# Where the two halves of P x V are joined and scaled: in the attention stage on VectorE and GpSimd, or in the output stage on GpSimd

## What is computed

```python
q = rmsnorm(x @ wq_a.T) @ wq_b.T              # 32 heads, 64 plain + 64 rotated
kv = rmsnorm(ckv) @ wkv_b.T                   # ckv has 64 columns
scores = einsum('bqhd,bkhd->bhqk', q_full, k_full) * softmax_scale
attn = softmax(where(causal, scores, min))
out = einsum('bhqk,bkhd->bqhd', attn, v)      # P x V
return out.reshape(B, S, H * VD) @ wo.T       # output product
```

## Time and profile before

| | before |
|---|---|
| median of three runs | 1893.46 us (1892.46 to 1895.08) |
| the profiled execution's own time | 1895.1 us (it is the longest of the three) |
| its span | 1895.1 us; nothing lies around it |
| TensorE busy (matmuls) | 1803.7 us, 95% |
| VectorE busy | 1231.4 us, 65% |
| ScalarE busy | 1000.5 us, 53% |
| GpSimd busy | 877.8 us, 46% |
| granted TensorE clock, mean | 0.985 |
| DMA | 182.74 MB, mean 96 GB/s |

### The profile page before, as it was taken

One profiled execution on the slowest core, in us unless ns is written; L12 is line 12 of the kernel. 1 busy time (PEld: TensorE's weight loads), 2 busy tenths in 40 slices (PEclk: granted clock), 3 DMA queues, 4 the chain that ended last, 5 costly groups with the idle time before them and its releaser, 6 DMA issues. The chain is left out here.

```text
span 1895.1 us, 44298 instructions
## 1 busy us (share of the span) xinstructions
PE 1803.7 (95%) x15472; PEld 1422.9 (75%) x15472; DVE 1231.4 (65%) x2654; ACT 1000.5 (53%) x2137; POOL 877.8 (46%) x641
## 2 busy tenths in 40 slices
PE   5999969899999999999999999998999999989999
PEld 4788869877777777777777777775788888877887
DVE  5655358688898888889888888989521111125453
ACT  2221047788887888888787888877310100112110
POOL 3232112377777878777787878775000000014321
PEclk9999979999999999999999999999999999989999
DMA  6542162311212112121222212123742233224321
GB/s 217 193 156 100 67 173 94 84 62 44 86 59 78 57 62 80 57 80 40 85 69 68 69 51 82 55 86 113 249 151 89 94 100 115 67 87 158 130 89 59
DMA packets 111969, 182.74 MB, mean 96 GB/s; under 512 B 27680, under 2 KB 64672, under 8 KB 109856
## 3 DMA queue, kind: packets, MB, share of 16 engines
q1 hardware_dynamic: 111904, 181.88, 29.8%
HBM read 122.33 MB, written 59.51 MB: 96 GB/s over the span
## 5 line engine op out<-in xcount | busy, mean ns | idle before, releaser
L1290 PE MATMUL psS<-keyT,q 128*128 128x512 f32 (+2 forms) x2304 | 473.2, 350 | 23.9 <-POOL q L648 14.5
L1290 PEld LDWEIGHTS psS<-keyT,q 128*128 128x128 f32 x2304 | 381.2, 189 | 118.2 <-DVE negmax L1408 41.7
L1357 ACT ACTIVATE prob<-prob,negmax 128x640 f32<-128x640 f32 (+7 forms) x512 | 392.0, 767 | 78.5 <-DVE negmax L1408 75.9
L1418 DVE STREAM_TRANSPOSE pT<-prob 128x640 f32<-128x640 f32 (+7 forms) x512 | 379.9, 762 | 66.4 <-PE psV L1307 61.6
L1408 DVE CUSTOM_DVE_ANT_0 prob<-psS,mask 128x640 f32<-128x640 f32 (+7 forms) x512 | 371.9, 742 | 20.9 <-PE psS L1290 7.4
L469 PE MATMUL f_psy<-f_weff,f_xT 128*128 128x512 f32 x1344 | 315.6, 393 | 0.0
L1101 PE MATMUL psS<-o_w,o_o 128*128 128x512 f32 x1344 | 304.8, 389 | 0.0
L469 PEld LDWEIGHTS f_psy<-f_weff,f_xT 128*128 128x128 f32 x1344 | 250.9, 188 | 55.8
L1101 PEld LDWEIGHTS psS<-o_w,o_o 128*128 128x128 f32 x1344 | 252.3, 188 | 52.4
L1307 PE MATMUL psV<-pT,val 32*64 32x512 f32 (+3 forms) x8192 | 264.8, 407 | 6.4 <-DVE pT L1418 6.2
L1307 PEld LDWEIGHTS psV<-pT,val 32*64 32x64 f32 x8192 | 168.8, 132 | 109.7 <-issue 66.2
(11 more groups left out here) (120 smaller groups left out, 1919.1 us busy)
## 6 DMA issues: line engine op xcount, KB each, us to landing
wo<-in_wo SPq DMA_DIRECT2D x16, 1024.0 KB, 6.0
pT<-row_scales SPq DMA_DIRECT2D x128, 128.0 KB, 2.9
oT<-pT SPq DMA_DIRECT2D x64, 256.0 KB, 2.5
o_in<-oT SPq DMA_DIRECT2D x32, 512.0 KB, 5.2
f_xt<-in_x SPq DMA_DIRECT2D x16, 512.0 KB, 4.4
f_w_in<-in_w SPq DMA_DIRECT2D x16, 512.0 KB, 6.7
w_sum<-f_w_in SPq DMA_DIRECT2D x16, 512.0 KB, 5.3
x<-f_xo SPq DMA_DIRECT2D x16, 512.0 KB, 3.0
```

The lines of the kernel that those rows point to most:

```text
L1290: ins = nc.tensor.matmul(psS[:, slot, start + x0:start + x1], q[:, e, a, t * P:(t + 1) * P], k.keyT[:, m, b * S + x0:b * S + x1], start=(i ...
L1357: nc.scalar.activation(row, row, ACT.Exp, bias=negmax[:, n % 8:n % 8 + 1], scale=-1.0, accum_out=rowsum[:, column(n, s):column(n, s) + 1]) ...
L1418: nc.vector.transpose(pT[:, n % 2, t, 0:width], prob[:, n % RING, 0:width]).then_inc(turned, 1)
```

## The change

P x V's banks are copied whole, all 128 partitions, by ScalarE into o_raw, now four quarters of pT's free part, and this signals `evicted`. The joins on VectorE, the scalings on GpSimd and the way of the scales back into o_scale go. SP stores both partial sums in parts_d, 4 x 256 KB a unit, and the scales in a table by token tile. In the output stage, SP loads for each half tile the lower partial sums into o_in, the upper ones and the scales (spread over 64 partitions) into the not yet used low and high part of the tile's o: 12 transfers of 256 KB a tile. GpSimd adds and multiplies (`join_outputs`), and signals ScalarE. A tile's loads wait for the tile before to be split and for the one before that to be multiplied. o_in moves to the place of cosT and sinT, x_in to that of wo. The output product goes through the pairs in order with both banks of a pair together; tiles 0 and 1 are no longer laced. ScalarE and VectorE split weights 0 to 4 ahead of tile 0's first half; SP loads tile 1's outputs behind weight 13. All other jobs of the attention stage keep their order.

```diff
@@ -897,9 +897,9 @@
 ACT_STEP = ("F0-1 F1-1 E8-1 Q0+0 E9-1 E10-1 Q1+0 E11-1 W0-1 H0+0 E12-1 E13-1 H1+0 E14-1 E15-1 Q2+0 Q3+0 E0+0 E1+0 E2+0 "
             "E3+0 E4+0 E5+0 E6+0 H2+0 E7+0 H3+0 O0-1 O1-1 O2-1 O3-1")
 DVE_STEP = ("M15-1 T12-1 T13-1 M0+0 T14-1 M1+0 M2+0 M3+0 T15-1 M4+0 M5+0 T0+0 R1-1 T1+0 T2+0 M6+0 T3+0 M7+0 T4+0 T5+0 "
-            "T6+0 R0+0 T7+0 O0-1 M8+0 O1-1 F0+0 M9+0 O2-1 T8+0 F1+0 M10+0 M11+0 T9+0 O3-1 M12+0 M13+0 T10+0 T11+0 "
+            "T6+0 R0+0 T7+0 M8+0 F0+0 M9+0 T8+0 F1+0 M10+0 M11+0 T9+0 M12+0 M13+0 T10+0 T11+0 "
             "M14+0")
-POOL_STEP = ("B2+0 B3+0 A0+1 A1+1 B0+1 B1+1 P0-1 P1-1 A2+1 A3+1")
+POOL_STEP = ("B2+0 B3+0 A0+1 A1+1 B0+1 B1+1 A2+1 A3+1")
...
-        self.o_in = at("o_in", "wo", 0, [P, PAIRS, P])
+        self.o_in = at("o_in", "cosT", 0, [P, PAIRS, P])
         self.o = [at("o_o0", "qnT", row * SLOTS, [P, 2, PAIRS, P], F32R), at("o_o1", "val", 0, [P, 2, PAIRS, P], F32R)]
-        self.x_in = [at("o_x_in0", "cosT", 0, [P, D]), at("o_x_in1", "sinT", 0, [P, D])]
+        self.x_in = [at("o_x_in0", "wo", 0, [P, D]), at("o_x_in1", "wo", row, [P, D])]
...
-    def load_outputs(self, sp, n):
+    def raw(self, j, part, h):
+
+        return self.o[j][:, part, self.half_of(h), :].bitcast(F32).rearrange("p a n -> p (a n)")
+
+    def load_outputs(self, sp, n, j, h):
+        x = slice(h * PAIRS * P // 2, (h + 1) * PAIRS * P // 2)
+        parts = self.parts_d.rearrange("(n e h v) m -> e h v n m", n=NT, e=2, h=2)[:, :, :, bass.ds(n, 1), x]
+        for e in range(2):
+            rows = slice(KVR * e, KVR * e + KVR)
+            even, odd = (parts[e, i].rearrange("v a m -> v (a m)") for i in range(2))
+            scale = self.scales_v[e, bass.ds(n, 1), x].to_broadcast([KVR, PAIRS * P // 2])
+            sp.dma_start(self.o_in[rows, self.half_of(h), :].rearrange("p a n -> p (a n)"), even).then_inc(self.o_loaded[h], 16)
+            sp.dma_start(self.raw(j, LO, h)[rows, :], odd).then_inc(self.o_loaded[h], 16)
+            sp.dma_start(self.raw(j, HI, h)[rows, :], scale).then_inc(self.o_loaded[h], 16)
+
+    def join_outputs(self, nc, pool, n, j):
         for h in range(2):
-            sp.dma_start(self.o_in[:, self.half_of(h), :], self.oT_v[:, self.half_of(h), bass.ds(n * P, P)]).then_inc(self.o_loaded[h], 16)
+            both = self.o_in[:, self.half_of(h), :].rearrange("p a n -> p (a n)")
+            pool.wait_ge(self.o_loaded[h], n * 96 + 96)
+            nc.gpsimd.tensor_tensor(both, both, self.raw(j, LO, h), ALU.add).then_inc(self.o_joined, 1)
+            pool.wait_ge(self.o_joined, n * 2 + h + 1)
+            nc.gpsimd.tensor_tensor(both, both, self.raw(j, HI, h), ALU.mult).then_inc(self.o_scaled, 1)
+
+    def pool_steps(self, nc, pool):
+        for n in range(2):
+            self.join_outputs(nc, pool, n, n)
+
+        def step(n, j, has):
+            if has(1) and later(n, 1):
+                self.join_outputs(nc, pool, n + 1, (j + 1) % 2)
+        output_steps(pool, step)
...
                 sp.wait_ge(self.o_lo, n * 2 + 2)
-                self.load_outputs(sp, n + 1)
+                sp.wait_ge(self.product, n * 2)
+                for h in range(2):
+                    self.load_outputs(sp, n + 1, (j + 1) % 2, h)
...
-        act.wait_ge(self.o_loaded[h], n * 16 + 16)
+        act.wait_ge(self.o_scaled, n * 2 + h + 1)
...
-            if pair in (0, 1, 8, 9):
-                self.outputs_hi(nc, act, pair // 8, pair // 8, pair % 2)
+            if pair in (5, 7):
+                self.outputs_hi(nc, act, 0, 0, pair // 7)
...
-        behind = 8
-        for p in range(PAIRS + behind):
-            for tile, pair in ((0, p), (1, p - behind)):
-                if not 0 <= pair < PAIRS:
-                    continue
-                pe.wait_ge(self.o_lo, 2 * tile + 2 * pair // PAIRS + 1)
-                pe.wait_ge(self.w_lo, pair + 1)
-                for half in range(2):
-                    x = slice(half * BANK, (half + 1) * BANK)
-                    for i, (a, m) in enumerate(PASSES):
-                        ins = nc.tensor.matmul(self.ps[:, tile, x], self.o[tile][:, a, pair, :], self.w[pair][:, m, x],
-                                               start=(pair == 0 and i == 0), stop=(pair == PAIRS - 1 and i == 2))
-                    if pair == PAIRS - 1:
-                        ins.then_inc(self.product, 1)
+        def add_pair(j, pair, closing):
+            for half in range(2):
+                x = slice(half * BANK, (half + 1) * BANK)
+                for i, (a, m) in enumerate(PASSES):
+                    ins = nc.tensor.matmul(self.ps[:, j, x], self.o[j][:, a, pair, :], self.w[pair][:, m, x],
+                                           start=(pair == 0 and i == 0), stop=(pair == PAIRS - 1 and i == 2))
+                if closing:
+                    ins.then_inc(self.product, 1)
+
+        for pair in range(PAIRS):
+            pe.wait_ge(self.o_lo, 2 * pair // PAIRS + 1)
+            pe.wait_ge(self.w_lo, pair + 1)
+            add_pair(0, pair, pair == PAIRS - 1)
+        for pair in range(PAIRS):
+            pe.wait_ge(self.o_lo, 2 * pair // PAIRS + 3)
+            add_pair(1, pair, pair == PAIRS - 1)
...
+                for pair in range(PAIRS):
+                    if pair % (PAIRS // 2) == 0:
+                        pe.wait_ge(self.o_lo, n * 2 + 2 * pair // PAIRS + 1)
+                    add_pair(j, pair, pair == PAIRS - 1)
...
-            def turn_scales(it, ch, s):
+            def store_scales(it, ch, s):
 
                 step, x = it * 2 + s, 2 * QT * (s % 2) + QT * ch
-                rows = rinv_d[bass.ds(step, 1), ch * S:(ch + 1) * S].rearrange("a (c q) -> (a c) q", q=P)
                 sp.wait_ge(r_turned, step * 2 + ch + 1)
                 for g in range(BLOCKS):
-                    if g == BLOCKS - 1 and later(step, 1):
-                        sp.wait_ge(scaled, step * 2 + ch - 1)
-                    sp.dma_start(rows[:, 32 * g:32 * g + 32], rinvT[32 * g + x:32 * g + x + QT, x // QT, :]).then_inc(r_stored, 16)
-                sp.wait_ge(r_stored, step * 128 + ch * 64 + 64)
-                for e in range(2):
-                    x = ch * S + e * CHUNK
-                    sp.dma_start(o_scale[KVR * e:KVR * e + KVR, ch, :],
-                                 rinv_d[bass.ds(step, 1), x:x + CHUNK].to_broadcast([KVR, CHUNK])).then_inc(r_loaded[ch], 16)
-
-            def store_o(it, ch, s):
+                    sp.dma_start(rinv_d[x:x + QT, bass.ds((it + s // 2) * P + 32 * g, 32)],
+                                 rinvT[32 * g + x:32 * g + x + QT, x // QT, :]).then_inc(r_stored[x // QT], 16)
+
+            def store_o(it, e, s):
                 b, pair = s % 2, it + s // 2
-                sp.wait_ge(scaled, (it * 2 + s) * 2 + ch + 1)
-                sp.dma_start(oT_d[bass.ds(pair * P, P), b * S + ch * CHUNK:b * S + (ch + 1) * CHUNK], o_raw[:, ch, :]).then_inc(o_stored[ch], 16)
+                sp.wait_ge(evicted, (it * 2 + s) * 4 + 4)
+                parts = parts_d.rearrange("(n e p) m -> e p n m", n=NT, e=2)[e, :, :, bass.ds(pair * P, P)]
+                for a in range(2):
+                    n = b * QT + a * QT // 2
+                    sp.dma_start(parts[:, n:n + QT // 2, :],
+                                 o_raw[:, 2 * e + a, :].rearrange("p (t q) -> p t q", q=P)).then_inc(o_stored, 16)
...
-                        sp.wait_ge(w_done, units)
-                        sp.wait_ge(o_stored[0], 16 * (units - 1))
-                        output.load_outputs(sp, 0)
+                        sp.wait_ge(queries.roped, 4 * units)
+                        for ch in range(2):
+                            sp.wait_ge(r_stored[ch], 64 * PAIRS)
+                        sp.wait_ge(o_stored, 64 * (units - 1))
+                        for h in range(2):
+                            output.load_outputs(sp, 0, 0, h)
                     if r.last and s == 1 and job == "Z":
-                        sp.wait_ge(output.o_lo, 2)
-                        output.load_outputs(sp, 1)
-                        output.load_weights(sp, range(SLOTS, 3 * SLOTS))
+                        output.load_weights(sp, range(SLOTS, 2 * SLOTS))
                     if r.last and s == 1 and (job, n) == ("X", 1):
-                        output.load_weights(sp, range(3 * SLOTS, PAIRS))
+                        sp.wait_ge(w_stored, 16 * units)
+                        output.load_weights(sp, range(2 * SLOTS, 3 * SLOTS))
             rounds(sp, body)
-            sp.wait_ge(w_stored, 16 * units)
-            for ch in range(2):
-                sp.wait_ge(o_stored[ch], 16 * units)
+            output.load_weights(sp, range(3 * SLOTS, 14))
+            sp.wait_ge(output.o_lo, 2)
+            output.load_outputs(sp, 1, 1, 0)
+            output.load_weights(sp, range(14, PAIRS))
+            output.load_outputs(sp, 1, 1, 1)
+            for slot in range(4):
+                sp.wait_ge(r_stored[slot], 64 * PAIRS)
+            sp.wait_ge(o_stored, 64 * units)
...
```

(23 more changed lines are left out.)

72 lines of the change are left out of this document (28 added, 44 removed).

## The result

The changed kernel takes 1927.56 us (median of 4 runs, 1926.77 to 1929.93) against 1893.05 beside it: a ratio of 1.0181, 95% interval 1.0167 to 1.0196. It is slower by 34.5 us where 41 us of gain were forecast. Its profiled execution spans 1925.0 us, 29.9 more than that of before.

A forecast was written before the change was run, and what follows sets the result against it. TensorE was taken to bound the kernel, so time could be won only where it pauses or runs slowly. 36 + 3.3 + 2.3 - 0.7 = 40.9 us off 1893.5 gave 1852.5 us, range for 8 in 10 1838 to 1886.

The forecast's parts named there:

- The chain of the output stage: Output stage: a tile's load, join and split take 19.1 us, 21.0 at worst, under TensorE's 21.8, so cost nothing.
- third rival: Output stage: a tile's 4.2 MB at one low mean rate; at 242 GB/s 69 us lost, about 1921 us; chance 0.10.
- the ring: Output stage: load, join, split, then the next tile's loads, as o_in frees only after the split; put at 19.1 us.
- The attention stage's gain: Attention stage: 1.2 us a unit, 36 us over 30 intervals; low end 14 us, high end 48.
- (a): Attention stage: from P x V's end to the first query product 1.92 us instead of 2.71; about 0.8 with folds.
- (b): Attention stage: without scaling GpSimd's rotation starts 1.1 us earlier, just in time; up to 0.4 us wait every second unit.
- (c): Attention stage: VectorE, with 3.3 us less work, takes later maxima at once; 0.4 us a unit, ends 0 and 0.8.
- The wider evictions: Attention stage: ScalarE's whole-bank evictions stay at 0.59 us each; bounded at -0.1 and +0.2 us each.
- The last P x V: Change of stages: VectorE's joins leave the stretch before the last P x V; 3.3 us won (2 to 4).
- Tiles 0 and 1: Change of stages: waits and slow clock 5 us instead of 7.3; 2.3 us won (8 lost to 5 won).
- The last half result: End of the output stage: one half result falls behind the last matmul; 0.7 us lost (0 to 1.5).
- the prediction's second page: Skill page on DMA row pitch, 164 GB/s at 2 MiB: a unit's store about 6 us, tile 0 some 3 us later.

The follow-up runs named there:

- e1_wide: Changed kernel, output-stage loads over 128 partitions, three of 512 KB a half tile, the two heads' data mixed: 1880.33 us.
- e7_split: e1_wide with each transfer cut in two by columns, again six of 256 KB a half tile: 1883.44 us.
- e16_before_halves: Kernel before, with each output load of a tile cut in two over the halves of the partitions: 1895.31 us.
- e17_half_wait: Changed kernel with SyncE's wait split, so a tile's first-half loads wait only for the first-half split of the tile before: 1887.54 us, ratio 0.9963.
- e9_thin_join: Kernel before, VectorE's joining after the first unit cut to 2 rows of 8 elements, GpSimd's scaling kept: 1886.03 us.
- e12_tuned: Whole version, parts loaded over 128 partitions, scales over 64; tile 1's first half before weights 12 to 15, tile 0's split one weight earlier: 1896.74 us.
- e15_order: e14_copies with all output weights loaded before tile 1's outputs, tile 0's first-half split before weight 4 instead of 5: 1890.95 us, ratio 0.9982.
- e14_copies: Changed kernel with rows stored in blocks of 128 and scale rows stored 8 times, so output loads fill 128 partitions: 1891.01 us, ratio 0.9985.

## Why the prediction was wrong

**The chain of the output stage is the step that failed.** It was put at 19.1 us, at worst 21.0, with the 373 GB/s of the earlier trace rows. Those loads filled 128 partitions; the new ones fill 64 and ran at 216. The term that failed is the landing of both halves: put at 10.4 us, it took 17.25. The rest of the chain held: 4.8 us for the joins behind the last load, 2.3 for the split, 24.6 with the short waits between. The third rival named this place and a low transfer rate, though not the 64 partitions, gave 1921 us for 242 GB/s, and had a chance of 0.10. That 1921 lies near the measured 1927.56 is luck: it put 69 us on the tiles, where 37.3 were lost, and kept the gains that failed to come elsewhere. Its formula was off in two ways that partly cancel: the rate was lower than the 242 that it priced, but a tile's tokens and results (1.05 MB) queue behind the second half and don't delay it. With 3.15 MB at 216 GB/s it gives 2.0 + 14.6 + 5.2 + 2.5 = 24.3. The argument against it, that the low means of the earlier trace rows hold idle time between loads, was not checked on a load of the new shape; the loads' partitions stood in the diff. e1_wide, e7_split and e16_before_halves show that the 64 partitions hold the rate down, e17_half_wait that the loss needs the ring as well: the same rate, 40 us less.

**The attention stage's gain was 0.64 us a unit, not 1.2.** The sum broke a limit that stood in the earlier trace rows: 21.2 us idle in 830, which are 27.4 units, allow 0.77 a unit as long as the work stays the same. Of its terms, (a) was right in the unit without folds (1.80 us from P x V to the first query product instead of 2.71) and half right in the one with folds, 3.61 instead of 3.98: a pause of 0.29 us that waits for nothing (13 times between 400 and 1270 us, once a pair, so probably at the turn of the loop) stood under the wait of 0.34 for GpSimd and came to light. (b), GpSimd just in time, held: no wait for it is left, and e9 shows that without its scalings gone there is one. (c), 0.4 us from VectorE's later maxima, was nothing: 18.61 and 18.77 us against 18.63 and 18.78 before. So 20 us came instead of 36, inside the stated ends of 14 and 48. The wider evictions cost nothing, as taken: 0.60 us each instead of 0.59.

**The last P x V** starts 5.87 us after its last scores instead of 6.22, and 2.0 us are won from unit 30 on, not 3.3. e9_thin_join, which thins the joins alone, has 26.4 us for that stretch, against 27.6 before and 25.6 in the changed kernel: 1.3 us come from the joins, which stood for the rest under TensorE's work.

**Tiles 0 and 1** were to win 2.3 us and lost 16.5: the waits and the slow clock, put at 5 us, came to 23.7. From the last P x V to tile 2 the kernel before needs 60.9 us and the changed one 77.4; e1_wide needs 69.1 and e7_split 68.2, so up to half of the loss goes with the rate. The whole versions with wide loads need 72 to 74 us, and e17_half_wait, at the slow rate, 73.6. Single profiles differ here by some 3 us: the stop for weight 14 is 9.21 us in the changed kernel and 5.90 in e17_half_wait, whose code is the same up to there. That weight is queued behind six of tile 1's loads. The 5.12 us stop before tile 0, which the kernel before didn't have, ends with VectorE's split of tile 0's first half (1315.37 to 1316.58 us). The prediction named the loss of the second tile that filled the gaps, but priced it at little. One thing it did not see is in VectorE's splits of the weights, changed kernel, ns min/median/max:

```profile
L1087 DVE TENSOR_TENSOR o_w<-o_w_in,o_w x12: 1183/1221/3381, 1300.2 to 1327.3; 128x1024 fp32r<-128x1024 f32 x12
```

The first four take 8.91 us together, from 1300.17, while GpSimd joins tile 0's first half; its two instructions take 2.90 and 3.23 us there and 2.35 for the second half. The prediction cited the Trainium skill's GPSIMD Engine Reference ("Key points") for this sharing, and looked only at what GpSimd would lose; VectorE lost too, some 4 us. No experiment separates this from the order of the loads; e12_tuned and e15_order show that reordering alone wins nothing there, the wait moves. That part is argued, not shown.

**The last half result** cost the 0.7 us it was put at. The stores, which by the prediction's second page would take 6 us a unit and bring tile 0 some 3 us later, landed in 3.0 us for 256 KB (median of 128); no run measures what they cost tile 0.

With the ring open the change gives 7 us by the ratio of e17_half_wait. Its last P x V starts 23.6 us earlier than before (1298.53 against 1322.11), and the passage to tile 2 takes 12.7 of them back (73.6 us against 60.9).

## What to carry to other kernels

Look first at how many partitions a new transfer fills and what its outermost dimension is: the rate of a row of the trace holds only for transfers of its shape. A transfer that is off the path by average traffic (19.4 us of a 21.8 us tile at 216 GB/s) can still set the pace through a single buffer that is waited for whole; write the ring down from issue to issue, and ask which wait in it can be taken half by half. And hold every sum of gains against the idle time of the engine that sets the pace.

## What the runs showed of the hardware

Loads over 64 partitions ran at 216 GB/s in one queue, about 243 with the halves alternating, about 270 from two queues. The same bytes over 128 ran at up to 447, though not all the time: the first four us of a tile's burst stayed at 164 to 343 in e1_wide, and more than half of a burst below 300 in e14_copies; why is open. A transfer with an outermost dimension of 2 ran at 51 GB/s. Side by side, a 128x1024 instruction of VectorE with two inputs took up to 3.38 us instead of 1.22, and GpSimd's up to 3.23 instead of 2.35.
